# Transposes of the next pair's x go into the bank of q, in the steps that set up no batch

## The reference

```
x = x + attention(layernorm(x), ctx)     # 16 heads of 64: q = ln(x) Wq, k = ctx Wk, v = ctx Wv, softmax, Wo, + bo
x = x + ffn(layernorm(x))                # silu(xq Wg^T) * (xq Wu^T), then a down projection, 704 hidden
# before each product of the ffn, its activations and its weights are rounded to fp4 in blocks of 16
```

## Time and profile before

| | |
|---|---|
| median of 3 runs | 917.21 us (916.43 to 921.49) |
| the profiled execution | 919.99 us, its span 918.2 us |
| mean granted TensorE clock | 0.979 |
| PE busy | 845.4 us (92%) |
| DVE busy | 714.5 us (78%) |

### The profile page before, as it was taken

The page is one execution under the profiler, slowest core; times in us unless marked ns, Lnnn a source line. Parts: engine busy times, 40 slices in busy tenths (PEclk is TensorE's granted clock), DMA queues, the critical chain, the costliest instruction groups (busy, mean ns, idle before and its releaser), DMA issues.

```text
span 918.2 us, 21455 instructions
## 1 busy us (share of the span) xinstructions
PE 845.4 (92%) x6254; PEld 807.5 (88%) x6254; DVE 714.5 (78%) x2157; ACT 523.8 (57%) x1878; POOL 539.8 (59%) x810
## 2 busy tenths in 40 slices
PE   4786899999999999989999999989999999999985
PEld 3666889999989999989988999989988999999874
DVE  5659788877777888867878888877877888887786
ACT  4544566566665655656655565556655565656531
POOL 6429676765446666646544666655644666666643
PEclk9989999999999999999999999999999999999996
DMA  7101000001000000001010000000100000000000
GB/s 239 47 12 44 7 19 13 24 7 47 14 30 25 12 25 10 19 16 41 13 36 19 14 24 13 23 9 14 47 7 19 12 25 13 12 16 13 7 6 17
DMA packets 20152, 23.22 MB, mean 25 GB/s; under 512 B 2659, under 2 KB 18251, under 8 KB 20043
## 3 DMA queue, kind: packets, MB, share of 16 engines
q1 hardware_dynamic: 20042, 21.94, 7.6%
HBM read 17.74 MB, written 4.19 MB: 24 GB/s over the span
## 4 chain that ended last, share of the span: by engine, by line
PE 64%; DVE 22%; issue 6%; ACT 4%; POOL 2%; DVEq 0%; ACTq 0%; POOLq 0%
PE ps_q L1156 9%; PE ps_s L1198 8%; PE ps_g L1241 8%; PE ps_t L1208 6%; PE ps_o L1221 5%; PE ps_o L1223 5%; PE ps_o L1222 5%; PE ps_g L1119 3%; DVE negmax L880 3%; DVE pT_lo L733 3%; DVE scales L760 3%; PE ps_m L1255 3%; PE ps_m L1257 2%; PE ps_m L1256 2%; ACT probs L674 2%
## 5 line engine op out<-in xcount | busy, mean ns | idle before, releaser
L507 POOL TENSOR_TENSOR probs<-probs,rsum 128x308 f32<-128x308 f32 x256 | 179.8, 703 | 270.3 <-DVE rsum L844 262.6
L674 ACT ACTIVATE probs<-ps_s,negmax 128x154 f32<-128x154 f32 x512 | 194.7, 386 | 223.3 <-DVE negmax L880 222.1
L880 DVE TENSOR_REDUCE negmax<-ps_s 128x2 f32<-128x308 f32 x256 | 121.0, 472 | 95.3 <-PE ps_s L1198 94.8
L1221 PE MATMUL ps_o<-B_sb,pT_lo 128*128 128x256 f32 x640 | 181.2, 283 | 0.9 <-DVE x_both L935 0.6
L1223 PE MATMUL ps_o<-B_sb,pT_hi 128*128 128x256 f32 x640 | 180.9, 283 | 0.0
L1222 PE MATMUL ps_o<-B_sb,pT_hi 128*128 128x256 f32 x640 | 180.6, 282 | 0.0
L733 DVE TENSOR_TENSOR pT_lo<-ps_t,pT_hi 128x256 fp32r<-128x256 f32 (+1 forms) x256 | 122.8, 480 | 34.0 <-ACT pT_hi L568 33.8
L1208 PE MATMUL ps_t<-ident,probs 128*128 128x128 f32 x640 | 113.9, 276 | 25.3 <-DVE pT_lo L733 22.4
L1241 PE MATMUL ps_g<-WGU,xqT_hi 128*128 128x352 f32 x504 | 132.1, 344 | 2.2 <-DVE B_sb L733 1.9
L1221 PEld LDWEIGHTS ps_o<-B_sb,pT_lo 128*128 128x128 f32 x640 | 121.3, 190 | 1.4 <-issue 0.8
L1223 PEld LDWEIGHTS ps_o<-B_sb,pT_hi 128*128 128x128 f32 x640 | 121.7, 190 | 0.0
(11 more groups left out here) (220 smaller groups left out, 2221.4 us busy)
## 6 DMA issues: line engine op xcount, KB each, us to landing
xa<-in_x_dram SPq DMA_DIRECT2D x33, 128.0 KB, 2.2
xr<-in_x_dram SPq DMA_DIRECT2D x32, 128.0 KB, 2.1
out_dram<-y_xn SPq DMA_DIRECT2D x30, 128.0 KB, 1.7
W_sb<-in_L_xattn_Wk_dram SPq DMA_DIRECT2D x4, 512.0 KB, 3.4
W_sb<-in_L_xattn_Wv_dram SPq DMA_DIRECT2D x3, 512.0 KB, 3.6
probs<-in_L_xattn_Wq_dram SPq DMA_DIRECT2D x2, 512.0 KB, 8.4
Wo_sb<-in_L_xattn_Wo_dram SPq DMA_DIRECT2D x1, 1024.0 KB, 9.4
VT<-in_L_ffn_w_down_dram SPq DMA_DIRECT2D x2, 352.0 KB, 3.7
```

The lines of the kernel that those rows point to most:

```text
L507: pool.tensor_tensor(unit, unit, rsum[:, 2 * u:2 * u + 2].unsqueeze(2) .to_broadcast([P, 2, M]), ALU.mult).then_inc(norm_p, 1)
L674: ins = act.activation(probs[:, h, 0:M], ps_s[k % 2][:, s * M:(s + 1) * M], ACT.Exp, bias=negmax[:, h:h + 1], accum_out=sums[:, h:h + 1])
L880: dve.tensor_reduce(negmax[:, 2 * k:2 * k + 2], ps_s[k % 2][:, 0:UM].rearrange("p (h m) -> p h m", h=2), AX_X, ALU.max, negate=True).then_ ...
L1221: pe.matmul(ps_o[:, 0:C], lo[:, j, :], w[:, 0:C], start=first, stop=False)
```

## The change

Where a step has no setup, `both_transposes` writes ps_q in place of ps_m, ACT and DVE read it from there, and the wait ahead of it is for the last q_lo of the pair in place of the last hqT_lo and `m_free`. In the same steps the down product no longer waits for xT_lo, but for hqT_lo, for which it waits anyhow. Steps with a setup, and the transposes ahead of the first step, are as before.

```diff
+        def xT_bank(setup):
+
+            return ps_m if setup else ps_q
...
-                        hi_part(xT_all(0), parts(ps_m, 4), (xT_mm, pair + 2), xT_hi)
+                        hi_part(xT_all(0), parts(xT_bank(setup), 4), (xT_mm, pair + 2), xT_hi)
...
-                        lo_part(xT_all(1), parts(ps_m, 4), xT_all(0), (xT_hi, pair + 2), xT_lo)
+                        lo_part(xT_all(1), parts(xT_bank(setup), 4), xT_all(0), (xT_hi, pair + 2), xT_lo)
...
-            def both_transposes():
+            def both_transposes(ps):
...
-                        ins = pe.transpose(ps_m[:, (2 * k + i) * P:(2 * k + i + 1) * P],
+                        ins = pe.transpose(ps[:, (2 * k + i) * P:(2 * k + i + 1) * P],
...
-                        m_free((hqT_lo, 2 * d + 2), (xT_lo, pair + 2))
-                        both_transposes()
+                        if xT_bank(setup) is ps_m:
+                            m_free((hqT_lo, 2 * d + 2), (xT_lo, pair + 2))
+                        else:
+                            pe.wait_ge(q_lo, PAIRS * (pair + 1))
+                        both_transposes(xT_bank(setup))
...
-                        down_product(d, (xT_lo, pair + 2) if par == 0 else (hqT_lo, 2 * d + 2))
+                        down_product(d, (xT_lo, pair + 2) if par == 0 and xT_bank(setup) is ps_m else (hqT_lo, 2 * d + 2))
```

More of the change, by code:

```diff
@@ L1170, in _ @@
             m_free(None, (xT_lo, 1))
-            both_transposes()
+            both_transposes(ps_m)
             pe.wait_ge(ld_ctx, 64)
```

## The result

The changed kernel takes 911.81 us in the median of seven runs (909.17 to 915.48), beside 916.43 us for the kernel before (915.77 to 921.49, seven runs). The medians lie 4.6 us apart. The ratio over all runs, which is not that of the two medians, is 0.9939, 95% interval 0.9918 to 0.9961: faster by 0.6%, which is 5.6 us. One execution of the kernel before, of 1638.18 us, stood apart from all others (the next slowest took 921.58) and is left out wherever its runs are counted. The forecast was 913.0 us, with "within 0.5%" as the likeliest case; the time lies in the range, the likeliest case did not come true.

What follows compares the result with a forecast made beforehand. PE was taken to set the pace, its down product standing behind DVE's xT_lo. Seven places at 0.60 us gave 4.2 us, all else nothing: 917.2 - 4.2 = 913.0 us, range 911.2 to 917.0 us.

Steps and rivals of the forecast that it cites:

- within 0.5%: Case that the measurement tells no difference from the kernel before, about 4.6 us either way; chance 0.65.
- The wait removed: Down product in slot 7 no longer waits for xT_lo: 0.60 us in each of seven places, 4.2 us in all.
- That it carries on: Slot 0 scores end 0.60 us earlier, DVE's slack falls from 0.95 to 0.35, and nothing is lost later; chance 0.74.
- Slot 6: Wait for hqT_lo ahead of the x transposes goes, 1.2 us idle in six places; gain costed at nothing.
- the rival that counted on this slot: Slot 6's wait counts too: 4.4 + 1.2 = 5.6 us won, 911.6 us; chance 0.04.
- The wait for q_lo, and the bank: Slot 6's added wait, q_lo ending 3.6 us ahead, and ps_m written while DVE reads ps_q: both cost nothing.
- The collision of L774 with POOL: Slot 0: DVE's L774 meets POOL's L528; taken as nothing, else 1.8 us lost, 914.8 us; within a 0.16 chance.
- The slower rival: Changed loop body makes PE stand at three inner-loop turns, 3 x 2.36 = 7.1 us, giving 920.1 us; chance 0.06.
- from the sum to the chances: Forecast 913.0 us against bound 912.6 us: faster 0.30, within 0.5% 0.65, slower by over 0.5% 0.05.

Runs made afterwards that it cites:

- keep_down_wait: Changed kernel with the x transposes still in the bank of q, but the down product waiting for xT_lo again; 916.74 us, ratio 0.9984 to before.
- keep_hqT_wait: Changed kernel whose x transposes in slot 6 also wait for hqT_lo as before, beside their new wait; 911.76 us, ratio 0.9936 to before.
- after_dve_late: Changed kernel plus one needless DVE reduction at the end of slot 7 in the eight changed places; 916.29 us, ratio 0.9996 to before.
- after_again: The changed kernel measured and profiled once more, with no edit; 911.28 us, ratio 0.9930 to before (0.9911 to 0.9949).
- v_steps_too: Changed kernel with the x transposes of the v steps (pairs 3, 7, 11) also in the bank of q; 911.70 us, ratio 0.9937 to before.
- unrolled pair: Kernels before and after, each with the outer loop over batches written out on the four compute engines; 909.52 and 905.06 us.
- both kernels with the needless reduction: Kernels before and after, each with one extra DVE reduction at the end of slot 7 in the eight changed places; 917.29 and 916.29 us.

## Why the prediction was right and wrong

The wait removed: right in place and kind. It was priced at 0.60 us and is worth 0.64. From the transposes to the down product it is now 0.28 us, 0.61 less than before; the other 0.03 lie in the down product, which has 2.24 us from its first matmul to the scores before, and 2.21 now. Why is open: in keep_down_wait it starts from a stand as well and has 2.21. I had read the distance up to the first matmul and not on to the scores behind; the par=1 steps of the kernel before, with no such wait, have 2.49 us from transposes to scores (pair 4, from 305.08 to 307.57) beside 3.13 in pair 5, and that difference is the 0.64.

```profile
305.08 0.52 PE L1208 MATMUL ps_t<-ident,probs 128*128 128x128 f32 x3
305.36 0.36 PE L1255 MATMUL ps_m<-WD,hqT_lo 128*128 128x256 f32 x1
...
307.57 0.30 PE L1198 MATMUL ps_s<-K_hi,q_lo 128*128 128x308 f32 x1
```

That it carries on: right. DVE's idle time ahead of the scores came out at 0.30, forecast 0.35, and each changed tile is shorter by the full 0.64. Putting this wait back alone takes all of it away.

Slot 6: right, with no gain. The trace after has the transposes of x 0.36 us behind those ahead of them, as before (0.37); the idle time that the view put down to hqT_lo is now put down to nothing, and has not gone. The measured 5.6 us is the very number of the rival that counted on this slot; that is chance, since neither the tiles nor keep_hqT_wait show any of its 1.2 us.

The wait for q_lo, and the bank: right at nothing; xT_lo takes 0.68 us as in the earlier trace rows with PE at work beside it.

The collision of L774 with POOL: it did not come. The two touch as the sum said (POOL's L532 runs from 332.23 to 332.96, DVE's instruction starts at 332.92), and the latter keeps its 0.89 us. But my bound for it was too low. I took the longest of the line, 0.47 above the median; with POOL first by 0.01 us it is 0.59. The Trainium skill ("SBUF — State Buffer", Who interferes with whom) has the rule behind that rival, that a DVE instruction with two SBUF inputs contends with a GpSimd instruction that reads SBUF. By that rule, the traces agree in both orders: POOL second in pair 1, DVE second in after_dve_late.

The slower rival, new stands where the inner loop turns back: it did not come. Between tiles 2 and 30 the trace after has the two stands on issue at the outer turns, 2.37 and 1.97 us, and no other.

**The step that failed** is the last one, from the sum to the chances. I set 4.2 us against a bound of 4.6 us and called "within 0.5%" the likeliest by 0.65, as if the measured difference were the path's. First, the term of the wait was too small by 0.3 us, so that the path alone gives 4.5 us, 0.49%, which the first interval of the ratio still holds (0.9951 in 0.9918 to 0.9961) and that of after_again does not (up to 0.9949). Second, I took the spread of the runs as a matter of the bound and named no case for it. The trace had it: PE stands at the outer loop's turn, and what the clock does behind that differs from execution to execution by up to 3.6 us. Over 79 executions of the kernel before and 13 of the changed one the means are 917.04 and 911.44 us, 5.6 apart, and the mean granted clocks 0.9829 and 0.9855. Within each kernel 0.001 of clock goes with 0.44 to 0.46 us, so this difference goes with 1.2 us, and 4.4 are left, which is the path. That is a correlation and no experiment, and a loose one: within the twelve runs of keep_down_wait the same 0.001 goes with 0.07 us, within the six of v_steps_too with 0.83. The unrolled pair, without turns, shows 4.4 us in the stretch and 4.5 in the medians, though its clocks differ the other way round (0.987 and 0.985), so the mean clock is a coarse measure.

Whether the change makes the higher clock likelier stays open. keep_down_wait speaks against a link with the gain: it has the clock of the changed kernel (0.985) and the path of the one before. The end of the program takes 87.2 us in both profiles of before and 86.0 to 86.1 in both of after. Up to the last maximum, 42.4 us behind that of tile 30, all traces agree to 0.1 us; what differs lies behind it, where the granted clock falls to 1.2 GHz in several places that are not the same in all executions (from 56 to 60 and from 60 to 64 us behind the maximum of tile 30 its mean is 0.88 and 0.69 in the first profile of before, 1.00 in both in that of after). That this is all of the difference is not shown. It doesn't go with the version alone: it is 86.5 in keep_down_wait, 86.95 in both kernels with the needless reduction, and 86.2 beside 85.9 in the unrolled pair.

## What to carry to other kernels

A wait is worth the distance between the instructions around it on the engine that sets the pace, less the same distance in a place where nothing waits, and both read on to the next engine's hand-over; the idle time that a view of waits reports was only 0.37 of 0.64 us here. A bank that two stages share can cost the later stage everything that stands between the first one's last write and its last reader; look for another bank whose last reader is long done. And where a gain is near the bound of the measurement, look for what moves between executions (here a loop's turn and the clock behind it), give it a case of its own, and measure by landmarks in the trace, which repeat to some hundredths of a microsecond.

## What the runs showed of the hardware

Where the outer loop turns back, PE stands for 1.8 to 2.4 us with nothing to wait for but its own issue, and then is granted 1.2 GHz for a part of the next microseconds in some executions and not in others (a mean granted clock of 0.69 against 1.00 over 4 us), which moves one tile from 27.9 to 29.5 us. The length of the stand does not decide it (1.97 us with, 2.30 us without). Writing the loop out removed both, and 7 us with them.

One more wait behind a late one can cost, even if its semaphore has long been set: 0.19 us ahead of the down product in keep_down_wait (1.08 against 0.89 us), 0.17 in the tile, in the six places inside the loops. In pair 2, which is written out ahead of them, it cost nothing (0.37 us of idle time, as before). What makes the difference is open.

Of a DVE instruction with two inputs in SBUF and a POOL instruction that reads SBUF, the one that starts second is held up and the first keeps its time: POOL second by 0.03 us, 1.44 us in place of 0.74; DVE second by 0.01 us, 1.47 in place of 0.88; DVE second by 0.35 us, 1.14 in place of 0.89.
